# One residual load ahead of four block loads, and one row maximum behind the next mask, in the opening of a graph-attention kernel

## What is computed

```
output = x @ weight;  q = x @ wq;  k = x @ wk
alpha  = q @ k.T                                  # 256 x 256 for each item
alpha  = maximum(alpha, 0) * (adj != 0)
alpha  = softmax(alpha, axis=1)
y      = alpha @ output
x      = layernorm(x + y)                         # no scale, no shift, eps 1e-5
```

## Time and profile before

| what | value |
|---|---|
| median of 3 runs | 520.11 us (519.36 to 520.21) |
| the profiled execution | 519.83 us |
| its span, first to last instruction | 518.0 us |
| PE busy | 510.5 us (99%) |
| DVE, ACT, POOL busy | 377.9, 331.0, 263.3 us |
| granted clock, mean | 0.997 |

### The profile page before, as it was taken

How to read it: one execution, slowest core, us unless ns; L and a number is a source line. 1 busy time by engine, 2 the same in 40 slices (tenths; PEclk the granted TensorE clock), 3 DMA queues, 4 the chain that set the end, 5 groups by cost and what they waited for, 6 DMA issues and landing times.

```text
span 518.0 us, 9835 instructions
## 1 busy us (share of the span) xinstructions
PE 510.5 (99%) x3212; PEld 464.4 (90%) x3212; DVE 377.9 (73%) x744; ACT 331.0 (64%) x756; POOL 263.3 (51%) x199
## 2 busy tenths in 40 slices
PE   8999999999999999999999999999999999999995
PEld 7888988899989998899988999889998999889995
DVE  5996776776848667586866778577694867757576
ACT  5855846386763857649474686638676385763677
POOL 0799784339526377145661486433953537710011
PEclk9999999999999999999999999999999999999998
DMA  8422151044510616024350332405342061501426
GB/s 293 159 76 83 47 199 61 20 129 158 197 66 20 223 61 243 20 71 172 125 198 19 123 141 110 174 20 172 112 180 84 20 222 61 202 1 36 167 90 236
DMA packets 30367, 62.05 MB, mean 120 GB/s; under 512 B 2064, under 2 KB 2320, under 8 KB 30352
## 3 DMA queue, kind: packets, MB, share of 16 engines
q1 hardware_dynamic: 30064, 61.48, 33.2%
q10 hardware_dynamic: 288, 0.39, 0.2%
HBM read 45.09 MB, written 16.78 MB: 119 GB/s over the span
## 4 chain that ended last, share of the span: by engine, by line
PE 96%; DVE 2%; DMA 1%; issue 0%; ACT 0%; POOLq 0%; POOL 0%; DVEq 0%; ACTq 0%
PE o_bank L349 12%; PE o_bank L350 12%; PE o_bank L351 12%; PE chain L349 11%; PE chain L351 11%; PE chain L350 11%; PE bank_y L349 6%; PE bank_y L350 6%; PE bank_y L351 6%; PE bank_z L351 3%; PE bank_z L349 3%; PE bank_z L350 3%; PE o_bank L576 1%; DMA xn<-in_wq_t 1%; PE o_bank L580 1%; PE o_bank L584 1%
## 5 line engine op out<-in xcount | busy, mean ns | idle before, releaser
L1595 POOL TENSOR_TENSOR s_lo<-xs,s_hi 128x512 fp32r<-128x512 f32 x56 | 76.9, 1388 | 36.0 <-ACT s_hi L760 36.0
L1590 POOL TENSOR_TENSOR a_lo<-xt,a_hi 128x512 fp32r<-128x512 f32 x42 | 57.0, 1366 | 61.9 <-ACT a_hi L752 61.9
L349 PE MATMUL o_bank<-t_hi,a_hi 128*128 128x256 f32 x256 | 72.6, 284 | 0.0
L350 PE MATMUL o_bank<-t_lo,a_hi 128*128 128x256 f32 x256 | 72.4, 283 | 0.0
L351 PE MATMUL o_bank<-t_hi,a_lo 128*128 128x256 f32 x256 | 72.4, 283 | 0.0
L1600 POOL TENSOR_TENSOR rstd<-var_eps,minus_half 128x4 f32<-128x4 f32 x14 | 14.3, 1019 | 92.3 <-DVE var_eps L1235 92.3
L783 ACT COPY parts<-chain 128x256 f32<-128x256 f32 x90 | 33.0, 369 | 37.0 <-PE chain L351 35.7
L1155 DVE TENSOR_TENSOR parts<-parts,bank_y 128x512 f32<-128x512 f32 x32 | 22.0, 688 | 42.6 <-ACT parts L769 25.5
L1221 DVE SCALAR_TENSOR_TENSOR xn<-o_bank,xn 128x512 f32<-128x512 f32 x62 | 42.5, 685 | 12.7 <-PE o_bank L351 11.9
L350 PE MATMUL chain<-w_lo,s_hi 128*128 128x256 f32 x180 | 50.9, 283 | 0.0
L351 PE MATMUL chain<-w_hi,s_lo 128*128 128x256 f32 x180 | 50.9, 283 | 0.0
(11 more groups left out here) (209 smaller groups left out, 1647.9 us busy)
## 6 DMA issues: line engine op xcount, KB each, us to landing
xn<-in_x SPq DMA_DIRECT2D x16, 1024.0 KB, 5.3
xt<-in_x_t SPq DMA_DIRECT2D x60, 256.0 KB, 3.0
out<-xn SPq DMA_DIRECT2D x14, 1024.0 KB, 5.2
adj<-in_adj_t SPq DMA_DIRECT2D x16, 512.0 KB, 4.6
xn<-in_wq_t SPq DMA_DIRECT2D x4, 256.0 KB, 4.1
xn<-in_w SPq DMA_DIRECT2D x4, 256.0 KB, 6.8
out<-xn SPq DMA_DIRECT2D x2, 512.0 KB, 3.3
parts<-in_wk_t SPq DMA_DIRECT2D x3, 256.0 KB, 4.8
```

Source lines behind the costliest of these rows:

```text
L349: nc.tensor.matmul(dst, a[0], b[0], start=first, stop=False, skip_group_check=shared)
L350: nc.tensor.matmul(dst, a[0], b[1], start=False, stop=False, skip_group_check=shared)
L1590: nc.gpsimd.tensor_tensor(a_lo[:, slot, u], xt[:, u], a_hi[:, slot, u].bitcast(F32), ALU.subtract).then_inc(a_lo_ready[slot], 1)
L1595: nc.gpsimd.tensor_tensor(s_lo[:, slot, s], xs[:, s], s_hi[:, slot, s].bitcast(F32), ALU.subtract).then_inc(s_lo_ready[slot], 1)
```

## The change

On SP the load of pair 1's residual goes out before the four block loads of pair 3 instead of between the second and the third of them. On DVE the maximum of row group 1 of pair 0 (`relu_max(0, 1)`) comes behind the second mask of pair 0, so behind two splits of t as well. On ACT the exponential that takes this maximum comes behind two splits of t. Nothing is added or left out.

```diff
@@ SP
             sp.wait_ge(gt_lo_ready, 4)
             load_xn(0, 0)
             load_adj(1)
-            load_b(1, A21)
-            load_b(1, A11)
 
             sp.wait_ge(wt_lo_ready, 4)
             load_xn(1, 1)
-            load_b(1, A12)
-            load_b(1, A22)
+            for u in (A21, A11, A12, A22):
+                load_b(1, u)
             group(1, first=True)
@@ ACT
             split_t_b(0, A11)
             split_t_b(0, A12)
             exponent(0, 0)
-            exponent(0, 1)
             split_t_b(0, A22)
             split_t_b(0, A21)
+            exponent(0, 1)
             exponent(0, 2)
             exponent(0, 3)
@@ DVE
             mask(0, 0, first=True)
             relu_max(0, 0)
-            relu_max(0, 1)
             split_t_b(0, A11)
             split_t_b(0, A12)
             mask(0, 1, first=True)
+            relu_max(0, 1)
             relu_max(0, 2)
             relu_max(0, 3)
             split_t_b(0, A22)
```

## The result

The changed kernel is slower by a little: median 520.35 us (22 runs) against 519.50 (22 runs of the kernel before), ratio 1.0017 with a 95% interval of 1.0010 to 1.0023, or +0.5 to +1.2 us. The prediction had 520.2 and a range of 519.2 to 520.9; its own working had +0.1 us, which is too small. Its 520.2 was added to a median of 520.11 from 3 runs, where the 22 runs have 519.50: that the two errors, 0.6 too high and 0.75 too low, nearly cancel in the time is luck.

What follows compares the result with a forecast made beforehand. PE was taken as the bound in opening and loop. Its 0.5 us delay was to vanish in the 0.67 wait before P1, leaving A11's 0.1: 520.11 + 0.1 = 520.2 us, range 519.2 to 520.9.

Steps and rivals of the forecast that it cites:

- The frame: PE bounds opening and loop; the change acts only between about 50 and 77 us, with at most 0.91 to win.
- Part 1: Moved maximum and exponential: PE 0.5 us late at the second half of pair 1's scores, bounds 0.1 and 0.5.
- The two rests: DVE's rests of t's A11 and A12, started 0.34 earlier, still end at 52.4 and 54.07, held by POOL.
- That place is the landing of block A11 of pair 3: ACT's 3.60 us wait for A11, up to 69.19, takes the 0.5 us delay without loss.
- the 0.5 passes through: Rival: A11 is issued and lands 0.5 late, chain and PE end 0.5 late, 520.6 us; chance 0.13.
- the residual's own time: Pair 1's residual, issued at 62.6, takes 4.9 to 5.3 us and lands at 67.5 to 67.9.
- The rival of the late blocks: Residual takes 7.0 us, lands at 69.6; A11 at 71.2, 2.0 late; time 522.1 us; chance 0.07.
- The first rival: A11 lands in 3.0 us, at 68.2, and the wait at 76.26 goes; 519.4 us at best; chance 0.14.
- the prediction's own signs: Right: A11's cast 69.1 to 69.5, P1's wait at most 0.3; wrong: cast before 68.9 or after 69.7.
- part 2: Reordered loads: residual goes out 2.6 us earlier, A11 lands at 69.1 to 69.5 against 69.2, middle 0.1 late.
- The sum: At P1 of t, PE's 0.5 falls into the 0.67 wait; A11's lateness leaves +0.1 us, bounds -0.2 and +0.3.

Runs made afterwards that it cites:

- e2: Only the maximum and the exponential moved, loads in the old order, against the kernel before: ratio 1.0008 (0.9997 to 1.0018).
- e11: Repeat of the kernel with only the maximum and the exponential moved, against the kernel before: ratio 1.0006 (0.9996 to 1.0015).
- e9: The full changed kernel once more, for a second profile, against the kernel before: ratio 1.0017 (1.0008 to 1.0026), median 520.78 us.
- e7: Kernel before, but POOL starts its three splits of weight sums only behind DVE's rests of t's A11 and A12: ratio 0.9996 (0.9987 to 1.0005).
- e1: Only the loads reordered, pair 1's residual ahead of pair 3's four blocks, against the kernel before: ratio 1.0014 (1.0005 to 1.0024).
- e3: Pair 1's residual loaded behind all four blocks of pair 3, otherwise the kernel before: ratio 0.9994 (0.9986 to 1.0003).
- e10: Repeat of the kernel with the residual loaded behind all four blocks, against the kernel before: ratio 0.9987 (0.9978 to 0.9996).
- e5: Maximum and exponential moved, and the residual loaded behind all four blocks, against the kernel before: ratio 0.9993 (0.9984 to 1.0002).
- e8: POOL's weight splits held behind DVE's two rests, and the residual loaded last, against the kernel before: ratio 0.9995 (0.9986 to 1.0004).

## Why the prediction was near and its sum too small

**The frame held.** PE is the bound, only the stretch up to P1 counts, and the loop gives nothing back: span minus P1's start is the same within 0.2 us in every profile.

**Part 1, up to PE: right, somewhat over-sized.** The forecast was PE 0.5 late at the second half of pair 1's scores, over one more exponential ahead of the reciprocal. e2, e11 and e9 have it 0.3 to 0.4 late, with the reciprocal idle for ACT by 0.37 to 0.38 where it was 0.22. The two rests did not end earlier for their earlier start (e2: the first began at 36.88 from G instead of 37.21 and ended at 38.49, where it ended at 38.46), and e7 shows why. The first profile of the changed kernel differs: there POOL's first split began behind DVE's rest of A11, the rests ended earlier, and no wait is seen at 57; its 43.64 comes from the late start at 49.97 instead.

**The step that failed: "That place is the landing of block A11 of pair 3: ACT waited 3.60 us for it, up to 69.19, and takes the 0.5 without loss."** The landing is not a fixed date. The block is issued when POOL has freed its place, POOL waits for ACT's casts, and those are the ones that part 1 delays (POOL's second split of a sum, which waits for ACT's cast, starts at 45.99 from G in e2 and at 45.59 before). The same paragraphs of the prediction had A11's issue 0.5 later, but let its landing be set by the residual alone. In e2 and e11, with the old order of loads, issue (+0.39 and +0.33), cast (+0.32 and +0.21) and P1 (+0.35 and +0.14) all move. This was the rival "the 0.5 passes through", which had 0.13. In the changed kernel itself it is the smaller share: A11 was issued 0.1 and 0.3 later than before, and took 0.7 and 1.0 us longer.

**The term that was mis-sized: the residual's own time.** 4.9 to 5.3 us were taken, from the earlier trace rows; it took 6.5 and 6.9 in the changed kernel and 6.1 in e1. A11 landed 1.2 to 1.3 behind it (1.6 were taken), at 69.7 and 70.7 in the raw times and at 70.0 and 70.5 when they are set to the zero of the profile before, instead of 69.1 to 69.5. The rows that the price came from had less behind them: at 114.92 one block was issued 1.7 us behind the residual and the next at 122.14, after it had landed. In the changed kernel two blocks follow within 2.6 us and a third after 5.0. The DMA view of the stretch from the residual's issue to its landing, at 114.92 in the profile before and then in e1, counts packets, MB and the share of the engines' time:

```profile
q1 hardware_dynamic: 651, 1.29, 71.6%
```

```profile
q1 hardware_dynamic: 806, 1.56, 74.9%
```

0.27 MB more, at the 390 to 420 GB/s that such a stretch reaches, are about 0.7 of e1's 1.2 us; this is an estimate from these rows. The prediction had seen that a transfer issued behind another slows it (A11's 1.5 us before) and did not apply it to the residual. The changed kernel moved 1.59 and 1.68 MB in its 6.5 and 6.9 us, so that some 0.8 and 1.0 of its 1.6 and 2.0 are of this kind; the rest is open. The rival of the late blocks (residual there at 69.6, A11 at 71.2) had the right direction, with a chance of 0.07: in e9 the residual was there at 69.6 and A11 at 70.7, in the first profile at 68.4 and 69.7. The price lay between the forecast's and this rival's. The first rival, that A11 goes in 3.0 us and the wait shrinks, fell: A11 took 4.8 to 5.5 behind the residual. By the prediction's own signs (A11's cast after 69.7, more than 0.3 of wait at P1) part 2 was read wrongly: the casts were at 69.67, just inside, and 70.81, and the wait was 0.86 in both profiles.

**The sum.** Taken together, P1 is 0.7 and 1.3 later in the two profiles than in the first before, about the +0.9 us of the times. e1 and e2 alone have +0.30 and +0.35 at P1 and +0.7 and +0.4 in time. How the sum divides between the two parts is known no better than to a few tenths: the parts' intervals overlap, e2's and e11's touch no change, and the residual's 6.1 to 6.9 us scatters by itself.

**What beats both.** The residual last (e3, e10): 519.15 and 519.21 us, the second next to 520.78 of the changed kernel on the same chip. Against the kernel before it is 0.9987 (0.9978 to 0.9996) in the second comparison and 0.9994 (0.9986 to 1.0003) in the first, which alone does not show it. The load is needed only in group 1, and the blocks are what PE waits for.

## What to carry to other kernels

A wait for a transfer absorbs a delay only if its issue doesn't hang on what is delayed: follow the issue back to the buffer's release before a stall is counted as slack. On a shared queue, order loads by who waits first, and price a load with its neighbours on both sides: a row of the steady loop is a price only where the same loads stand behind it. Where the bound engine never idles behind a place, one number (span minus that place's start) shows at once whether anything else has changed.

## What the runs showed of the hardware

- A 256 KB load took 3.2 to 3.3 us with nothing large near it (e3, e10, e5), 4.4 to 4.5 with 1024 KB issued 0.4 to 0.5 us behind it (before, e2, e11), and 4.8 to 5.5 with 1024 KB issued 2.5 us ahead (e1, the changed kernel). A later transfer on the same queue so cost an earlier one 1.2 us, and an earlier one cost a later one 1.5 to 2.2. With POOL held the block took 5.5 and 4.7 (e7, e8) for a reason that no run shows.
- DVE's subtraction of two SBUF tensors (128x512) took 0.66 to 0.69 us with POOL idle and up to 1.78 when it started inside a POOL instruction. How far POOL's instruction had got decided it: in the opening the rest of t's A21 began 1.07 us behind the start of a POOL sum of 1.29 in the profile before and took 0.78, and began 0.33 us behind that start in the changed kernel and took 1.50, which moved PE's next start by 0.7. The opening's phase itself (PE's first matmul into bank_y at 13.2 to 14.4) differs from execution to execution, which may be a part of why one kernel's times scatter by 2 us; this was not tried.
